# DLRM tower on one core: one-hot steps over 512 columns of four tiles, integer compare of ids, the last chunk in an order of its own

## The chip, the cores and the metric

One core of a Trainium2 chip. The metric is device time in microseconds (us) of one execution. TensorE is called PE (PEld is its weight load), VectorE DVE, ScalarE ACT, GpSimd POOL, SyncE SP. The program runs all engines side by side; they meet at semaphores only.

## The reference

```python
# ids: 2048 samples x 26 tables; 10 of the tables have 1000 rows ("one-hot" here), 16 others
# have 1250 to 125000 rows; every row has 128 float32
e = jnp.stack([tbl_0[ids[:, 0]], ..., tbl_25[ids[:, 25]]], axis=1)   # 2048 x 26 x 128
combined = jnp.concatenate([e, r_dense_x[:, None, :]], axis=1)       # 2048 x 27 x 128
z = jnp.einsum('bfd,bgd->bfg', combined, combined)[:, I, J]          # the 351 pairs f < g
h = jnp.concatenate([z, r_dense_x], axis=1)                          # 2048 x 479
h = jnp.maximum(h @ W_top1 + b_top1, 0.0)                            # 479 x 512
h = jnp.maximum(h @ W_top2 + b_top2, 0.0)                            # 512 x 256
y = h @ W_top3                                                       # 256 x 1
```

## The kernel before

The 2048 samples are 16 tiles of 128, and a chunk is two tiles (256 samples); there are 8 chunks, c = 0 to 7. Tile n is tile t of chunk c with n = 2c + t.

**Gathered tables.** For the 16 large tables POOL issues one indirect DMA per tile and table (`gather`, L242), 256 in all, into one of three row buffers. They are issued in halves of a tile (8 DMAs); from the sixth half on, half b waits until PE has done the half b - 4 of the pair products (`s_gpart`), and the first few halves wait for counts of used one-hot units (`LEAD`). PE turns four tables at a time over the diagonal (`turn`, L521, four transposes: a "turn"), and ACT copies each turn into `xt` (`evac_group`, L360). Turn g = 0 to 3 of a tile needs the landing of the tile's gathers 4g to 4g + 3.

**One-hot tables.** The ten small tables lie in SBUF whole, as a float32r high part (ACT, `high`) and a low part (DVE subtraction, `low`, L304). Their rows are fetched by matmul: partition p holds rows 8p to 8p + 7, ACT turns the chunk's ids (int32, broadcast to 128 partitions by DMA) into `id - 8p` as float (`shift_ids`), DVE compares that with k = 0 to 7, which makes one "unit" each (`make_units`, L279, 128x512 for a pair of tables by 256 samples), and PE multiplies table slices by the units into one of three PSUM banks `ps_lk` (`lookup`, L509: 8 values of k, 2 tables, 2 parts = 32 matmuls of 256 columns for a pair). The first lookup (L489) uses the raw float32 table. Five pairs make a chunk. Eight units are the ring; DVE may overwrite two of them when the matmuls that used them are done (`s_unit_used`). ACT copies each bank to `xt` (`evac_pair`, L350).

**Pair products and the MLP.** `gram` (L536) makes the 27x27 products of a tile in two halves of 64 samples, with 64 short matmuls (128 records) a half; DVE transposes and packs them (`pack`, L287 to L295); PE transposes the pairs (`turn_pairs`, L549), ACT copies them to `zt` (`evac_zt`). `layer1` (L562), `layer2` (L569), `layer3` (L577) follow for the whole chunk, in the next chunk's loop; in the last chunk `last1`, `last2`, `last3` (L590, L597, L605) do it tile by tile.

Every engine's order is written out by hand. In PE's loop for chunk c stand: pair transposes of chunk c-1, turn 3 of tile 2c, layer 3, lookups 3 and 4, layer 1, `gram` of tile 2c, lookup 0 of chunk c+1, the turns of tile 2c+1 between layer 1 parts, lookup 1 of c+1, layer 2, `gram` of tile 2c+1, with turns 0 to 2 of tile 2c+2 and lookup 2 of c+1 among it.

Of the kernel before, what the change touches and what calls it, by code (L numbers as in the profile page):

```python
# [13 lines left out]
P = 128  # L14
# [4 lines left out]
CT = 2  # L19
CHUNKS = TILES // CT  # L20
CS = CT * P
Q = 32
# [11 lines left out]

DENSE = 26
# [6 lines left out]
ROW_BUFS = 3  # L42
# [9 lines left out]
MLP_USES = T1 + T2 + 1  # L52


LP = NO // 2
LB = 3

RING = 8
UNITS = LP * KT
USE = 2  # L60
assert PAIRS == NF * (NF - 1) // 2 and NO % 2 == 0 and RING == KT and KT % USE == 0

CUT = (0, 4, NO)
# [3 lines left out]
LEAD = (0, 2, 8, 14, 20)  # L67

SPLIT = list(range(2, NO)) + [0, 1]
# [4 lines left out]
def build(nc, t_, out):  # L74
    ctx = ExitStack()
    with ctx:
# [11 lines left out]
        xt = sb("xt", [P, CS, NF])  # L88
        dense_x = sb("dense_x", [P, CS])
        ids = [sb(f"ids{h}", [P, CUT[h + 1] - CUT[h], CS], I32) for h in range(2)]  # L90
        ids_from = sb("ids_from", [P, NO, CS])
        onehot = sb("onehot", [P, RING, 2, CS], F32R)
        table = sb("table", [P, NO, 2, KT, D], F32R)
        first_i = sb("first_i", [P, 1], I32)
        first = sb("first", [P, 1])
# [16 lines left out]
        RAWS = len(stage) - 2  # L112
        raw = [stage[j] if j < 2 else stage[2 + (j - 2) % RAWS] for j in range(NO)]

        ps_lk = [pb(f"ps_lk{i}", [P, 2, CS]) for i in range(LB)]
        ps_tr = pb("ps_tr", [P, 512])
# [5 lines left out]
        s_ids = [sem(f"s_ids{h}") for h in range(2)]  # L122
        s_from = sem("s_from")
        s_ids_a = sem("s_ids_a")
        s_from_a = sem("s_from_a")
# [10 lines left out]
        s_first = sem("s_first")  # L136
# [18 lines left out]
        s_carrier = {e: sem(f"s_carrier_{e}") for e in ("dve", "pool", "sp")}  # L155

        def bank(c, i):
            return ps_lk[(c * LP + i) % LB]

        def mlp_bank(n):  # L160
            return (ps_mlp, ps_zt)[n % 2]

        def last1_bank(t, j):
            return ps_lk[j][:, 0, 0:P] if j < LB else (ps_tr, ps_mlp)[t][:, 0:P]

        def last2_bank(t, j):
            return ((ps_tr, ps_zt)[j][:, 0:P], ps_lk[j][:, 0, 0:P])[t]

        def last3_bank():
            return ps_lk[2][:, 0, :]  # L170
# [4 lines left out]
        def _(sp):  # L175
            def load_first_ids():
                sp.dma_start(ids[0][:, 0:2, :].rearrange("p a s -> p (a s)"),
                             t_["ids_onehot"][0:1, 0:2 * CS].to_broadcast([P, 2 * CS])).then_inc(s_ids_a, 16)
# [4 lines left out]
            def load_ids(c, h):  # L183
                if c > 0:
                    sp.wait_ge(s_from, (c - 1) * 2 + h + 1)
                    sp.sem_inc(s_carrier["sp"], 1)
# [537 lines left out]
```

## Time and profile before

| | us |
|---|---|
| median of 3 runs (lowest, highest) | 373.63 (371.1, 375.01) |
| the profiled execution, its own time | 374.13 |
| its span, first to last instruction | 371.9 |
| PE busy | 345.5 (93%) |
| POOL busy | 258.8 (70%) |
| ACT busy | 184.4 (50%) |
| DVE busy | 170.1 (46%) |

The span lies 2.23 us under the time of its own execution. Busy shares are means over the whole span; a gap of an engine counts only where something later waits for it. The page does not count the time in which POOL prepares the next issue as busy.

### The profile page before, as it was taken

Reading aid. Unit: us, or ns where it says so; the run is one execution under the profiler, and the core shown is the slowest. Engines: PE = TensorE matmul, PEld = TensorE weight load, DVE = VectorE, ACT = ScalarE, POOL = GpSimd, SP = SyncE. Lnnn points to the kernel's source line nnn. Section 1 sums busy time; section 2 is a strip of 40 time slices with the busy share of each in tenths; the row PEclk is TensorE's granted clock in tenths of the full one; section 3 lists DMA queues with packets and bytes.
Section 4 is the critical chain, followed back from the end, with each engine's and each line's share of the span. In section 5 each row is a group of like instructions: output and inputs, shape, how many; then the busy total and the mean of one; then the engine's idle time right before and its main releaser. Section 6 shows DMA issues by size and latency. Waiting matters only on the chain.

```text
span 371.9 us, 13580 instructions
## 1 busy us (share of the span) xinstructions
PE 345.5 (93%) x6176; PEld 317.1 (85%) x6176; DVE 170.1 (46%) x380; ACT 184.4 (50%) x235; POOL 258.8 (70%) x265
## 2 busy tenths in 40 slices
PE   1998787989998999999999999999999999999997
PEld 0898776879897889999899998999899998899887
DVE  4589654533533435356245535356244635350220
ACT  3588242764345543473716643473725734376433
POOL 6688877777777777777777777777777777774000
PEclk9999899999998999999999999999999999999999
DMA  7967743211622126221262226321262222221000
GB/s 242 356 183 243 232 149 107 67 51 51 196 70 67 51 58 183 78 65 51 68 198 53 65 54 173 91 67 53 51 206 60 64 53 65 55 56 37 19 4 3
DMA packets 15917, 37.14 MB, mean 100 GB/s; under 512 B 5141, under 2 KB 7829, under 8 KB 15860
## 3 DMA queue, kind: packets, MB, share of 16 engines
q0 software_dynamic: 8192, 16.79, 16.9%
q1 hardware_dynamic: 7668, 19.48, 16.1%
q8 instruction: 49, 0.80, 0.9%
q14 instruction: 8, 0.07, 0.1%
HBM read 36.24 MB, written 0.01 MB: 97 GB/s over the span
## 4 chain that ended last, share of the span: by engine, by line
PE 69%; POOL 20%; issue 7%; DMA 3%; SPq 0%; ACT 0%
PE ps_lk L509 29%; POOL rows L242 20%; PE ps_gram L536 10%; PE ps_tr L521 6%; PE ps_zt L562 6%; PE ps_mlp L562 6%; PE ps_mlp L569 3%; PE ps_zt L569 3%; DMA zt<-in_tbl 2%; PE ps_mlp L577 1%; PE ps_lk L590 1%; PE ps_lk L489 1%; PE ps_zt L549 1%; DMA rows<-in_tbl,gather_ids 1%; PE ps_lk L597 0%
## 5 line engine op out<-in xcount | busy, mean ns | idle before, releaser
L242 POOL DMA_INDIRECT rows<-in_tbl,gather_ids x256 | 257.4, 1006 | 80.4 <-issue 76.2
L279 DVE TENSOR_SCALAR onehot<-ids_from 128x512 fp32r<-128x512 f32 x320 | 126.3, 446 | 94.1 <-PE ps_lk L509 68.7
L509 PE MATMUL ps_lk<-onehot,table 128*128 128x256 f32 x1248 | 163.3, 290 | 2.6 <-DVE onehot L279 2.0
L509 PEld LDWEIGHTS ps_lk<-onehot,table 128*128 128x128 f32 x1248 | 155.9, 196 | 4.3 <-issue 3.1
L360 ACT COPY xt<-ps_tr 128x512 f32<-128x512 f32 x64 | 77.0, 1203 | 93.0 <-PE ps_tr L521 91.2
L536 PEld LDWEIGHTS ps_gram<-xt 128*26 128x26 f32 x4096 | 44.1, 103 | 23.4 <-issue 20.7
L536 PE MATMUL ps_gram<-xt 128*26 128x26 f32 x4096 | 52.7, 192 | 9.8 <-issue 4.8
L350 ACT COPY xt<-ps_lk 128x512 f32<-128x512 f32 x40 | 48.9, 1236 | 14.5 <-PE ps_gram L536 10.5
L287 DVE STREAM_TRANSPOSE zs<-ps_gram 128x832 f32<-128x832 f32 x16 | 16.8, 1050 | 85.9 <-PE ps_gram L536 85.9
L521 PE MATMUL ps_tr<-ident,rows 128*128 128x128 f32 x256 | 39.3, 276 | 3.3 <-ACT xt L360 1.8
L521 PEld LDWEIGHTS ps_tr<-ident,rows 128*128 128x128 f32 x256 | 29.6, 140 | 7.1 <-ACT xt L360 2.4
L562 PE MATMUL ps_zt<-zt,w 128*128 128x256 f32 (+1 forms) x112 | 26.5, 379 | 0.0
L562 PE MATMUL ps_mlp<-zt,w 128*128 128x256 f32 (+1 forms) x112 | 26.5, 379 | 0.0
L562 PEld LDWEIGHTS ps_mlp<-zt,w 128*128 128x128 f32 (+1 forms) x112 | 20.2, 190 | 2.2
L562 PEld LDWEIGHTS ps_zt<-zt,w 128*128 128x128 f32 (+1 forms) x112 | 20.2, 190 | 2.2
L345 ACT ACTIVATE ids_from<-ids,first 128x1536 f32<-128x1536 int32 (+1 forms) x15 | 20.5, 1367 | 1.3 <-DMA ids<-in_ids_onehot 1.3
L377 ACT ACTIVATE h<-ps_mlp,cols 128x256 f32<-128x256 f32 x7 | 3.3, 474 | 27.0 <-PE ps_mlp L569 27.0
L489 PE MATMUL ps_lk<-onehot,h 128*128 128x256 f32 x16 | 6.3, 483 | 8.3 <-DMA h<-in_tbl 8.3
L365 ACT COPY zt<-ps_zt 128x256 f32<-128x256 f32 x16 | 6.5, 407 | 14.6 <-PE ps_zt L549 14.6
L569 PE MATMUL ps_mlp<-h,w 128*128 128x256 f32 x56 | 13.3, 380 | 0.1
L569 PE MATMUL ps_zt<-h,w 128*128 128x256 f32 x56 | 13.3, 381 | 0.0
L304 DVE TENSOR_TENSOR table<-w,table 128x1024 fp32r<-128x1024 f32 x8 | 9.6, 1217 | 4.7 <-ACT table L334 4.7
(57 smaller groups left out, 153.7 us busy)
## 6 DMA issues: line engine op xcount, KB each, us to landing
ids<-in_ids_onehot SPq DMA_DIRECT2D x8, 768.0 KB
w<-in_tbl SPq DMA_DIRECT2D x8, 512.0 KB, 5.0
rows<-in_tbl,gather_ids POOLq DMA_INDIRECT x256
ids<-in_ids_onehot SPq DMA_DIRECT2D x7, 512.0 KB
dense_x<-in_dense SPq DMA_DIRECT2D x8, 128.0 KB
zt<-in_dense SPq DMA_DIRECT2D x8, 128.0 KB
ids<-in_ids_onehot SPq DMA_DIRECT2D x2, 256.0 KB, 4.1
h<-in_tbl SPq DMA_DIRECT2D x1, 512.0 KB, 5.9
```

The lines of the kernel that those rows point to most:

```text
L242: pool.indirect_dma_start(rows[n % ROW_BUFS][:, r, :], None, t_[f"tbl_{GATHERED[r]}"], bass.IndirectOffsetOnAxis(ap=gather_ids[:, n, r:r + ...
L279: nc.vector.tensor_scalar(onehot[:, u % RING, :, :], ids_from[:, 2 * i:2 * i + 2, :], float(k), None, ALU.is_equal).then_inc(s_unit, 1)
L287: nc.vector.transpose(zs[:, :, :], ps_gram[:, :, 0:GS].rearrange("p s g -> p g s")).then_inc(s_zs, 1)
L345: nc.scalar.activation(ids_from[:, CUT[h]:CUT[h + 1], :], ids[h][:, :, :], ACT.Identity, bias=first[:, :]).then_inc(s_from, 1)
L350: nc.scalar.copy(xt[:, :, NG + 1 + 2 * i:NG + 3 + 2 * i].rearrange("p s f -> p f s"), bank(c, i)[:, :, :]).then_inc(s_lk, 1)
L360: nc.scalar.copy(xt[:, t * P:(t + 1) * P, a:a + n].rearrange("p s f -> p f s"), ps_tr[:, 0:n * P].rearrange("p (f s) -> p f s", f=n)).then ...
L489: m = nc.tensor.matmul(bank(0, 0)[:, j, :], raw[j][:, k, :], onehot[:, k, j, :].bitcast(F32), start=(k == 0 and j == 0), stop=(k == KT - 1 ...
L509: m = nc.tensor.matmul(bank(c, i)[:, j, :], table[:, 2 * i + j, part, k, :], onehot[:, u % RING, j, :], start=(k == 0 and j == 0 and part ...
L521: i = nc.tensor.transpose(ps_tr[:, k * P:(k + 1) * P], rows[n % ROW_BUFS][:, r, :], ident[:, :])
L536: i = nc.tensor.matmul(ps_gram[q * Q:q * Q + GS, s, 0:GS], xt[:, x, 0:GS], xt[:, x, 1:NF], start=True, stop=True)
L562: i = nc.tensor.matmul(mlp_bank(j)[:, 0:CS], w1[0:r, k, j * P:(j + 1) * P], zt[0:r, k, :], start=(k == 0), stop=(k == NZ))
L569: i = nc.tensor.matmul(mlp_bank(T1 + j)[:, 0:CS], w2[:, k, j * P:(j + 1) * P], h1[:, k, :], start=(k == 0), stop=(k == T1 - 1))
```

## The change

A step now covers one table for four tiles (512 samples: `XT` = 4 tiles, `N` = 512 columns) instead of two tables for two tiles. Two sets of five tables alternate: chunk 0 makes FIRST for tiles 0 to 3 and, in three narrower steps, SECOND for tiles 0 and 1 (8 steps); chunk 1 makes SECOND for tiles 2 to 5, chunk 2 FIRST for tiles 4 to 7, and so on (5 steps each); chunk 7 has the three narrower SECOND steps alone. That is 41 steps of 8 units against 40. A wide step has 16 matmuls of 512 columns. `xt` holds four tiles, the row buffers are two instead of three. DVE compares the int32 ids with a float32 number per partition, `own[:, k]` = 8p + k, so ACT's shifts and `ids_from` are gone. The ids come in one DMA of 256 KB per step into four buffers; SP waits for the units of step e - 4 before it issues ids e. In the first chunk each step is preceded by the `high` and `low` of the next table or tables only. In chunk 7, layer 2 of chunk 6 and the last chunk's first tile are moved ahead of turn 3 of tile 15.

```diff
+CT = 2
+CS = CT * P
+XT = 2 * CT
+N = XT * P
+FIRST, SECOND = list(range(HALF)), list(range(HALF, NO))
+BY_CHUNK = [tuple(SECOND[i:i + 2]) for i in range(0, HALF, 2)]
+    if c == 0:
+        STEPS += [(c, XT, (i,)) for i in FIRST] + [(c, CT, b) for b in BY_CHUNK]
+    elif c == CHUNKS - 1:
+        STEPS += [(c, CT, b) for b in BY_CHUNK]
+    else:
+        STEPS += [(c, XT, (i,)) for i in (SECOND if c % 2 else FIRST)]
...
-ROW_BUFS = 3
+ROW_BUFS = 2
...
-LEAD = (0, 2, 8, 14, 20)
+LEAD = (0, 2, 6, 12, 20)
...
+            def load_ids(e):
+                if e >= IDS:
+                    sp.wait_ge(s_unit, (e - IDS + 1) * KT)
+                    sp.sem_inc(s_carrier["sp"], 1)
+                sp.dma_start(ids[e % IDS][:, :], t_["ids_onehot"][e:e + 1, :].to_broadcast([P, N])
+                             ).then_inc(s_ids[e % IDS], 16)
...
             sp.dma_start(gather_ids[:, :, :], ...).then_inc(s_gids, 16)
+            load_ids(0)
+            load_raw(0)
+            load_raw(1)
+            load_ids(1)
+            load_raw(2)
+            load_ids(2)
+            load_raw(3)
+            load_ids(3)
+            load_raw(4)
+            for e in range(IDS, IDS + 4):
+                load_ids(e)
+                load_raw(e + 1)
...
-            pool.iota(first_i[:, :], pattern=[[0, 1]], base=0, channel_multiplier=-KT).then_inc(s_const, 1)
+            pool.iota(own_i[:, :], pattern=[[1, KT]], base=0, channel_multiplier=KT).then_inc(s_const, 1)
...
-                    nc.vector.tensor_scalar(onehot[:, u % RING, :, :], ids_from[:, 2 * i:2 * i + 2, :],
-                                            float(k), None, ALU.is_equal).then_inc(s_unit, 1)
+            def make_units(e):
+                dve.wait_ge(s_ids[e % IDS], (e // IDS + 1) * 16)
+                for k in range(KT):
+                    if k % USE == 0 and e > 0:
+                        dve.wait_ge(s_unit_used, ((e - 1) * KT + k) // USE + 1)
+                    w = STEPS[e][1] * P * len(STEPS[e][2])
+                    nc.vector.tensor_scalar(onehot[:, k, 0:w], ids[e % IDS][:, 0:w], own[:, k:k + 1], None, ALU.is_equal
+                                            ).then_inc(s_unit, 1)
...
+            make_units(0)
+            for e in range(1, STEP0[1]):
+                for n in range(len(STEPS[e][2])):
+                    low(STEPS[e][2][n] - 1)
+                make_units(e)
...
+            def evac(e):
+                _, w, tables = STEPS[e]
+                a, f = NG + 1 + tables[0], len(tables)
+                act.wait_ge(s_unit_used, (e + 1) * KT // USE)
+                if w == XT:
+                    nc.scalar.copy(xt[:, :, a], ps_lk[e % LB][:, :]).then_inc(s_lk, 1)
...
+                    for j, i in enumerate(tables):
+                        x = slice(j * w * P, (j + 1) * w * P)
                         for part in range(2):
+                            m = nc.tensor.matmul(ps_lk[e % LB][:, x], table[:, i, part, k, :], onehot[:, k, x],
+                                                 start=(k == 0 and j == 0 and part == 0),
+                                                 stop=(k == KT - 1 and part == 1), skip_group_check=True)
...
+            lookup(5)
+            lookup(6)
+            turn(1, 0)
+            lookup(7)
+            e = STEP0[1]
+            gram(0, 0)
+            lookup(e)
+            turn(1, 1)
+            gram(0, 1)
+            turn(1, 2)
+            turn(1, 3)
+            gram(1, 0)
+            lookup(e + 1)
+            gram(1, 1)
+            lookup(e + 2)
...
...
+            c, a, e = CHUNKS - 1, TILES - 2, STEP0[-2]
+            turn_pairs(a - 2)
+            turn(a, 3)
+            layer3(c - 2)
+            lookup(e + 1)
+            turn_pairs(a - 1)
+            lookup(e + 2)
+            layer1(c - 1, 0)
+            gram(a, 0)
+            turn(a + 1, 0)
+            layer1(c - 1, 1)
+            turn(a + 1, 1)
+            layer1(c - 1, 2)
+            gram(a, 1)
+            layer1(c - 1, 3)
+            turn(a + 1, 2)
+            layer2(c - 1, 0)
+            layer2(c - 1, 1)
+            turn_pairs(a)
             layer3(c - 1)
             last1(0, 0)
             last1(0, 1)
+            turn(a + 1, 3)
+            gram(a + 1, 0)
             last1(0, 2)
+            gram(a + 1, 1)
             last1(0, 3)
+            last2(0, 0)
+            turn_pairs(a + 1)
+            last2(0, 1)
             for j in range(T1):
                 last1(1, j)
+            for j in range(T2):
+                last2(1, j)
             last3()
```

## Rows read from the trace of the kernel before

**Rows 1.** The page: busy tenths of two engines in 40 slices.

```profile
PE   1998787989998999999999999999999999999997
...
POOL 6688877777777777777777777777777777774000
```

**Rows 2.** The page, costliest groups: gathers, one-hot units, lookups, group copies, id shifts.

```profile
L242 POOL DMA_INDIRECT rows<-in_tbl,gather_ids x256 | 257.4, 1006 | 80.4 <-issue 76.2
...
L279 DVE TENSOR_SCALAR onehot<-ids_from 128x512 fp32r<-128x512 f32 x320 | 126.3, 446 | 94.1 <-PE ps_lk L509 68.7
...
L509 PE MATMUL ps_lk<-onehot,table 128*128 128x256 f32 x1248 | 163.3, 290 | 2.6 <-DVE onehot L279 2.0
...
L360 ACT COPY xt<-ps_tr 128x512 f32<-128x512 f32 x64 | 77.0, 1203 | 93.0 <-PE ps_tr L521 91.2
...
L345 ACT ACTIVATE ids_from<-ids,first 128x1536 f32<-128x1536 int32 (+1 forms) x15 | 20.5, 1367 | 1.3 <-DMA ids<-in_ids_onehot 1.3
```

**Rows 3.** The timeline of POOL: gathers 8, 9, 240 and 256 of 256.

```profile
12.40 0.95 POOL L242 DMA_INDIRECT rows<-in_tbl,gather_ids  x1 [0.30 <-issue]
...
15.19 0.94 POOL L242 DMA_INDIRECT rows<-in_tbl,gather_ids  x1 [1.85 <-PE ps_lk L489]
...
318.47 0.94 POOL L242 DMA_INDIRECT rows<-in_tbl,gather_ids  x1 [0.30 <-issue]
...
338.95 0.94 POOL L242 DMA_INDIRECT rows<-in_tbl,gather_ids  x1 [0.30 <-issue]
```

**Rows 4.** The chain in order of time (start, us, what): a landing, a lookup, layer 2.

```profile
111.75 2.93 DMA rows<-in_tbl,gather_ids
...
142.34 3.83 PE ps_lk L509 x32
...
315.63 1.73 PE ps_mlp L569 x8
```

**Rows 5.** The timeline of PE: fourth transposes of tiles 4, 14 and 15.

```profile
114.81 0.63 PE L521 MATMUL ps_tr<-ident,rows 128*128 128x128 f32 x4 [1.53 <-DMA rows<-in_tbl,gather_ids]
...
328.24 0.60 PE L521 MATMUL ps_tr<-ident,rows 128*128 128x128 f32 x4
...
348.54 0.60 PE L521 MATMUL ps_tr<-ident,rows 128*128 128x128 f32 x4
```

**Rows 6.** The timeline of the start: units, first lookup, subtractions, a gather, a slow lookup.

```profile
6.15 2.97 DVE L279 TENSOR_SCALAR onehot<-ids_from 128x512 fp32r<-128x512 f32 x8 [4.08 <-ACT ids_from L338]
...
8.26 1.19 PE L489 MATMUL ps_lk<-onehot,h 128*128 128x256 f32 x2 [8.26 <-DMA h<-in_tbl]
...
25.52 2.35 DVE L304 TENSOR_TENSOR table<-w,table 128x1024 fp32r<-128x1024 f32 x2
...
26.73 1.97 POOL L242 DMA_INDIRECT rows<-in_tbl,gather_ids  x1 [0.30 <-PE ps_lk L509]
...
41.45 5.38 PE L509 MATMUL ps_lk<-onehot,table 128*128 128x256 f32 x32 [0.71 <-DVE onehot L279]
...
46.76 1.69 PE L536 MATMUL ps_gram<-xt 128*26 128x26 f32 x128
```

**Rows 7.** Busy time by stretch: stretch, length, PE busy, granted clock, DMA share, GB/s.

```profile
42.00:44.00 2.00, 2.00 (x12) 0.50 0.91 276
```

**Rows 8.** The timeline of the last 24 us, PE, ACT and DVE.

```profile
349.27 1.99 PE L569 MATMUL ps_mlp<-h,w 128*128 128x256 f32 x8
...
351.19 1.27 PE L536 MATMUL ps_gram<-xt 128*26 128x26 f32 x128
...
356.65 1.05 DVE L287 STREAM_TRANSPOSE zs<-ps_gram 128x832 f32<-128x832 f32 x1 [7.93 <-PE ps_gram L536]
...
358.40 0.40 DVE L295 COPY_PREDICATED packed<-lower,zs 128x169 f32<-128x169 int32 x1
...
361.53 2.84 PE L590 MATMUL ps_lk<-zt,w 128*128 128x128 f32 x24
...
368.67 1.23 PE L605 MATMUL ps_lk<-cols,h 128*128 128x1 f32 x8
```

More of the change, by code:

```diff
@@ L52 @@
 MLP_USES = T1 + T2 + 1
[L55 removed]
+assert PAIRS == NF * (NF - 1) // 2 and NO % 2 == 0
+RING = KT
+USE = 2
 LB = 3
[L58 to L63, printed above, removed]
+IDS = 4
 PARTS = 2
[L67 to L69 removed]
+LEAD = (0, 2, 6, 12, 20)
+SPLIT = list(range(1, NO)) + [0]
 LAST = (CHUNKS - 1) * MLP_USES
@@ L121, in build @@
         s_gids = sem("s_gids")
[L122 to L125, printed above, removed]
+        s_ids = [sem(f"s_ids{b}") for b in range(IDS)]
         s_densex = sem("s_densex")
@@ L329, in _ @@
+            make_units(STEP0[-2] + 2)
+            pack(TILES - 2)
+            pack(TILES - 1)
         @block.scalar
@@ L389, in last_relu2 @@
             def last_relu2(t, j):
-                act.wait_ge(s_mlp, LAST + CT * T1 + t * T2 + j + 1)
+                act.wait_ge(s_mlp, last(t) + T1 + j + 1)
                 nc.scalar.activation(h2[:, j, t * P:(t + 1) * P], last2_bank(t, j), ACT.Relu,
                                      bias=cols[:, T1 + j:T1 + j + 1]).then_inc(s_act, 1)
-            act.wait_ge(s_first, 1)
-            nc.scalar.activation(warm[:, :], first[:, :], ACT.Identity)
-            shift_first(0, 2, s_ids_a, s_from_a)
@@ L413, in _ @@
-            shift_ids(1, 0)
-            evac_group(0, 1, 0)
-            evac_group(0, 1, 1)
-            shift_ids(1, 1)
-            evac_group(0, 1, 2)
-            evac_group(0, 1, 3)
+            act.wait_ge(s_own, 1)
+            nc.scalar.activation(warm[:, :], own[:, 0:1], ACT.Identity)
+            high(0)
+            high(1)
+            evac(0)
+            evac_group(0, 0)
+            high(2)
+            evac(1)
+            high(3)
+            evac(2)
+            evac_group(0, 1)
@@ L482, in lookup_first @@
             def lookup_first():
+                pe.wait_ge(s_raw[0], 16)
                 for k in range(KT):
                     pe.wait_ge(s_unit, k + 1)
-                    for j in range(2):
-                        if k == 0:
-                            pe.wait_ge(s_raw[j], 16)
-                        m = nc.tensor.matmul(bank(0, 0)[:, j, :], raw[j][:, k, :], onehot[:, k, j, :].bitcast(F32),
-                                             start=(k == 0 and j == 0), stop=(k == KT - 1), skip_group_check=True)
+                    m = nc.tensor.matmul(ps_lk[0][:, :], raw[0][:, k, :], onehot[:, k, :].bitcast(F32),
+                                         start=(k == 0), stop=(k == KT - 1))
@@ L677, in _ @@
             last1(0, 1)
-            turn_pairs(c, 1)
+            turn(a + 1, 3)
+            gram(a + 1, 0)
             last1(0, 2)
+            gram(a + 1, 1)
             last1(0, 3)
+            last2(0, 0)
+            turn_pairs(a + 1)
+            last2(0, 1)
             for j in range(T1):
                 last1(1, j)
-            for t in range(CT):
-                for j in range(T2):
-                    last2(t, j)
+            for j in range(T2):
+                last2(1, j)
             last3()
```

475 lines of the change are left out of this document (226 added, 249 removed).

## The prediction

> **What bounds the kernel now.** I read the page first: PE is at nine tenths or more nearly throughout, POOL at seven to eight tenths until it stops at some 340 us [rows 1]. The grouped rows [rows 2] correct the second: POOL's 256 gathers are 257.4 us busy and have 80.4 us of idle time before them, 76.2 of it under "issue", which is no wait for anybody. So POOL works for 257.4 + 76.2 = 333.6 us, as much as PE's 345.5. Its timeline says the same: apart from 1.85 us ahead of the ninth gather it never stands, and the last one starts at 338.95 [rows 3]. From gather 80 at 111.75 [rows 4] to gather 240 at 318.47 [rows 3] lie 160 gathers in 206.7 us, 1.292 us each, 41.3 us for a chunk of 32.
>
> How far is PE behind? A gather's rows land 2.93 us after its start [rows 4]. Turn 3 of tile 4 waits 1.53 us for them at 114.81. Turn 3 of tile 14 comes at 328.24 [rows 5], its rows are there at 318.47 + 2.93 = 321.4; turn 3 of tile 15 comes at 348.54, its rows at 341.9. PE needs (328.24 - 114.81) / 5 = 42.7 us a chunk against POOL's 41.3, and by the end it is 6.8 us behind. So at most about 7 us can be had from PE's lookups before POOL takes over, and what follows the last rows has to be counted by itself.
>
> **The change part by part.**
>
> *Wider lookups.* 32 lookup matmuls of 256 columns take 3.83 us [rows 4], 119.7 ns each; 256 columns at 2.4 GHz are 106.7, so 13 are on top. If the 13 belong to the instruction, 512 columns take 226 ns; if they go with the columns, 239; if the weight load hides wholly, 213. A step of 16 then takes 3.62 us (3.41 to 3.83), and a chunk of five saves 1.0 us (0 to 2.1). I take the middle. The Trainium skill ("TensorE: Matmul & The Clock Gate", Back-to-back issue gap) gives a warm gap of N/2.4 + 2.5 ns, 216 ns for 512 columns, which would save 1.9 us a chunk; the 119.7 measured here for 256 columns is 10 over that rule, so I don't lean on it. It doesn't matter much, as the sum shows.
>
> *Moved lookups.* Chunk 7's first five tables come with chunk 6's four-tile steps. PE's loop 6 loses two lookups (7.7 us), loop 7 half a lookup (1.9 us), and chunk 0 gains two and a half. There PE waits anyway: 1.53 us at tile 4 in the end, and for DVE and ACT before.
>
> *Start.* One 256 KB id load fewer lies ahead of the first raw table, so the first matmul starts some 0.7 us before the 8.26 of now [rows 6], and DVE doesn't wait for ACT's shift. The ninth gather waits for half of the first lookup; now that costs 1.85 - 0.3 = 1.5 us [rows 3], and the new first lookup needs one table instead of two (now it stops a second time for the other). I put POOL 1.3 us earlier. Then the steps: a DVE set of eight units is 2.97 us, two subtractions 2.35 [rows 6]. Steps 1 to 4 cost DVE 4.2 us each, 5 and 6 some 5.4, 7 about 3.5, against 3.6, 3.8 and 1.9 on PE; from 17.6 us PE gets through lookup 7 at about 44.6, the first `gram` from 46 to 48, one lookup, and the second half ends near 54 (now 48.4 [rows 6]). POOL's sixth half, near 60, waits for it: 6 us of room. Entering loop 1 PE is 1 us later than now and at tile 4's turn 3 still ahead of its rows, having 1.5 us to spare now plus a loop of saving. Cost: nothing; with that cover gone, each us late is a us on POOL.
>
> *POOL.* Its instructions are the same; the third row buffer was not used as such, since half b waits for half b - 4 before and after. Subtractions lengthen gathers (1.97 us where two of them run [rows 6], 0.94 otherwise); their number stays, and 328 unit operations instead of 320, more of them early, may add 0.5 us.
>
> *DVE's compare.* int32 input and a per-partition number in place of float and an immediate. A unit of 512 elements is 2.97 / 8 = 371 ns [rows 6], while a subtraction takes 1175 ns for 1024 elements, so the compare goes at a faster rate than one element in the subtraction's time; no row shows this operation with an int32 input. Lower bound 371 (it reads as many bytes), upper the subtraction's rate, half of 1175 ns and up to 90 ns of fixed cost that doesn't halve, 590 to 680 for 512 (an estimate). I take 371: the nearest row is the same instruction on words of the same size. "VectorE: DVE Perf Modes" (What auto-detection actually checks) in the Trainium skill names source count, place and outer size for the two-port mode, not the type, and so sides with 371; no row here shows it.
>
> *ACT* loses its id shifts (20.5 us and two small ones [rows 2]); it stands 91 us waiting for PE's turns, so that is worth nothing to the end. SP's id loads wait for units four steps back; the raw tables 6 to 9 are queued behind them, but are issued when their buffers come free anyway, some 5 us before they are used.
>
> *Loop 7 and the end.* Turn 3 of tile 14 waits for rows: 321.4 - 1.3 + 0.5 + 0.1 = 320.7. In every case of the lookup price PE is there first: it needs five chunks of 42.7 from 114.8, less 7.7 and 5 savings of 0 to 2.1 (two steps fewer in the last), at 312 to 320.6. From there to the end of turn 2 of tile 15 the work is that of now less half a lookup: 20.3 - 1.9 = 18.4 us. New ahead of turn 3 of tile 15: 0.23 until layer 1's last activation is done, layer 2 twice 1.75 [rows 4], 0.75 for its activation (now hidden behind `gram`), pair transposes and layer 3 1.2, two parts of `last1` 1.8: 7.5. That gives 25.9. PE idles some 5 to 8 us of the 12 before. In the trace of now the first `gram`, whose PE had waited just before, is followed by a stretch at clock 0.50 [rows 7], that is 1.2 GHz, in which a lookup takes 5.38 us [rows 6], some 1.3 more than undisturbed; after a longer idle time I add 1.5.
>
> After turn 3 of tile 15: transposes and the ACT copy until `gram` 2.0; `gram`, `last1` part, `gram` 1.2 + 0.9 + 1.2 [rows 8]; DVE's pack from its transpose at 356.65 to the last copy's end at 358.8 [rows 8], 2.15, and 0.25 to notice the `gram`; pair transposes and ACT copies 1.5 with their hand-overs; `last1` for tile 15 four times 0.9; activation 0.75; `last2` 1.8 [rows 8]; from there to the end as now, 371.9 - 368.67 = 3.2 [rows 8]. Sum 18.6, plus 0.8 for a clock drop that may follow the idle 1.5 us.
>
> Total: 320.7 + 25.9 + 1.5 + 18.6 + 0.8 = 367.5, against a span of 371.9: -4.4. The profiled execution took 374.13, so 369.7; its time lies 0.5 above the median of 373.63, which gives **369.2**.
>
> **The rivals.** *POOL has less to fight* (0.15): fewer gathers meet DVE's early subtractions (spread singly now), no clock drop in loop 7 or the tail. Each of the two is worth 2 to 3 us: 364 to 367. For it speaks that 1.292 a gather stands over the 0.94 + 0.30 = 1.24 of an undisturbed one [rows 3]; against it, that DVE's operations are as many as before.
>
> *The compare runs at one element per cycle* (0.10), the slower side. Units take 650 ns, eight of them 5.2 us. DVE then sets chunk 0: step 7's units end near 57, the next set near 63, the second half of the first `gram` near 65, 5 us after POOL wants it, and PE reaches tile 4 some 13 us later than now. Later loops hold 26 us of units in 41 and lose about 1 us each, so tile 14 comes at 327 instead of 320.7, and the time is 369.2 + 6.5 = 376, to 380 if POOL's delay adds. It decides from a unit of about 500 ns, where chunk 0's slack is used. The "GPSIMD Engine Reference" of the Trainium skill says that VectorE's two-port operations contend with GpSimd; by that, POOL would run faster at the same time, which only softens this case.
>
> *The last order costs more than it hides* (0.25): PE runs the 7.5 us of layer 2 and `last1` ahead of turn 3 while its rows, landed at 341, wait until 346.6. If the clock stays down longer, or the hand-overs of the tail (each 0.2 to 0.75, six of them) are dearer, 2 to 4 us go: 371 to 373, no change. *It doesn't matter where the lookups are* because PE is late at tile 4: would need 5 us more in chunk 0 than I count; it is within the case before.
>
> **How the numbers follow.** Main case 0.50, 367 to 371 with 369.2 the likeliest. 0.15 lies at 364 to 367, 0.25 at 371 to 373, 0.10 at 376 to 380. The range of 8 in 10 goes from 365 to 375. One per cent is about what a measurement of this kernel tells from no change: under 369.9 fall most of the better half of the main case and the first rival, 0.15 + 0.37 = 0.52; within one per cent 0.40; over 377.4 0.08.
>
> **What would show it.** Unit near 371 ns; a 512-column matmul 213 to 239 ns apart; gathers still 1.29 us apart, the last one near 338; PE's waits for rows at turns 1 to 3 of tile 14, some 8 us together or less; turn 3 of tile 15 near 348, 5 us after its rows; 19 us from there to the end. I am wrong if POOL waits for `gram` in the first 70 us, if units take over 500 ns, or if POOL's spacing moves by 2%.

## The result and the profile after

| | before | after |
|---|---|---|
| median of 4 runs (lowest to highest), us | 374.32 (371.1 to 645.01) | 385.86 (385.28 to 388.19) |
| span of the profiled execution, us | 371.9 | 383.5 |
| turn 3 of tile 14 / of tile 15, start | 328.24 / 348.54 | 330.65 / 357.88 |
| last gather, start | 338.95 | 347.76 |

One of the four runs before took 645.01 us, far off the others (371.1 to 375.01), and the ratio leaves it out. The ratio is 1.0335, 95% interval 1.0294 to 1.0376: slower by 3.3%, where 369.2 us was forecast, and outside the range of 365 to 375. The page of the kernel after, its parts 2 (40 slices), 4 (the chain that ended last) and 5 (groups: instructions and busy time, mean ns, idle time before them and its releaser), beside [rows 1] and [rows 2]:

```profile
POOL 6788877777777777777777777777777777772000
PEclk9999995999998799999999999999999998999959
...
POOL 60%; issue 19%; PE 17%; DMA 2%; ACT 1%; DVE 0%; SPq 0%
...
L262 POOL DMA_INDIRECT rows<-in_tbl,gather_ids x256 | 267.8, 1046 | 78.9 <-issue 77.1
L297 DVE TENSOR_SCALAR onehot<-ids,own 128x512 fp32r<-128x512 int32 (+1 forms) x328 | 141.8, 490 | 80.5 <-PE ps_lk L547 72.2
...
L558 PE MATMUL ps_tr<-ident,rows 128*128 128x128 f32 x256 | 41.2, 285 | 10.9 <-DMA rows<-in_tbl,gather_ids 9.5
```

POOL is the bound: the chain runs along its gathers for 79% of the span (60 + 19 "issue"). They are the same 256 as before, but the mean is 1046 ns instead of 1006 [rows 2]. The last starts 8.8 us later. Of that 6.2 us are lost early: the first 32 take 53.9 us from the first one's start to the 33rd's, against 47.7. The other 2.6 us come in the 223 gathers after that, 1.303 us apart against 1.292, where DVE makes units and no subtractions any more. At the end of its gathers the chain passes from POOL to PE here (its pieces: start, us, what), and PE's timeline says the same: at turn 3 of tile 14 it had waited 1.54 us for rows.

```profile
327.67 2.84 DMA rows<-in_tbl,gather_ids
330.51 0.14 issue
330.65 0.63 PE ps_tr L558 x4
```

The early loss has a place. POOL's timeline of the kernel after, 28 to 40 us (start, us, instruction, idle before it):

```profile
28.95 1.28 POOL L262 DMA_INDIRECT rows<-in_tbl,gather_ids  x1 [0.30 <-PE ps_lk L547]
30.53 3.55 POOL L262 DMA_INDIRECT rows<-in_tbl,gather_ids  x1 [0.30 <-issue]
34.39 1.28 POOL L262 DMA_INDIRECT rows<-in_tbl,gather_ids  x1 [0.30 <-issue]
35.98 3.55 POOL L262 DMA_INDIRECT rows<-in_tbl,gather_ids  x1 [0.30 <-issue]
```

and DVE's over the same time:

```profile
27.65 3.25 DVE L297 TENSOR_SCALAR onehot<-ids,own 128x512 fp32r<-128x512 int32 x8
30.82 1.21 DVE L303 TENSOR_TENSOR table<-zt,table 128x1024 fp32r<-128x1024 f32 x1
31.96 1.22 DVE L303 TENSOR_TENSOR table<-w,table 128x1024 fp32r<-128x1024 f32 x1
33.09 3.25 DVE L297 TENSOR_SCALAR onehot<-ids,own 128x512 fp32r<-128x512 int32 x8
36.26 2.35 DVE L303 TENSOR_TENSOR table<-w,table 128x1024 fp32r<-128x1024 f32 x2
```

Eight units take 3.25 us, 406 ns each, against 371 [rows 6]. A gather that begins 0.29 us before two subtractions takes 3.55 us. In the kernel before, the gather that begins 0.19 us before two of them (at 25.33; its line stands under "Open" below) takes 1.09, and only the next, which begins within the second, takes 1.97 [rows 6]. The long one ends at 30.53 + 3.55 = 34.08, and the subtractions end at 31.96 + 1.22 = 33.18: 0.90 us later, as long as an undisturbed gather lasts (0.94). From one set of units to the next DVE takes 33.09 - 27.65 = 5.44 us, and POOL the same from one long gather to the next (35.98 - 30.53 = 5.45). In that time it gets two gathers out, where undisturbed, at 0.94 + 0.30 us each, it would get four.

The wide lookups do what they were to do, at the dear end. PE's timeline in the middle of the run (x16 are the 16 matmuls of a step):

```profile
212.92 3.92 PE L547 MATMUL ps_lk<-onehot,table 128*128 128x512 f32 x16
216.67 1.90 PE L600 MATMUL ps_mlp<-zt,w 128*128 128x256 f32 x8
```

A step is 216.67 - 212.92 = 3.75 us, 234 ns a matmul, against 3.83 for 32 narrow ones [rows 4].

The end of the program, PE's timeline from turn 3 of tile 15 (the last number is the idle time before the group and its releaser):

```profile
357.88 0.60 PE L558 MATMUL ps_tr<-ident,rows 128*128 128x128 f32 x4
359.78 1.21 PE L573 MATMUL ps_gram<-xt 128*26 128x26 f32 x123 [1.30 <-issue]
363.09 0.24 PE L573 MATMUL ps_gram<-xt 128*26 128x26 f32 x5 [2.10 <-issue]
363.26 1.18 PE L628 MATMUL ps_lk<-zt,w 128*128 128x128 f32 x8
364.38 1.59 PE L573 MATMUL ps_gram<-xt 128*26 128x26 f32 x115
366.82 0.39 PE L573 MATMUL ps_gram<-xt 128*26 128x26 f32 x13 [0.85 <-issue]
367.14 2.08 PE L628 MATMUL ps_mlp<-zt,w 128*128 128x128 f32 x8
```

Within each half of the pair products PE stands and waits for no semaphore that the trace shows ("issue"), 2.10 and 0.85 us. And the clock falls after the first of these pauses; windows of the same stretch (length, busy of PE, PEld, DVE, ACT, POOL, then the granted clock as a share of 2.4 GHz, DMA share, GB/s):

```profile
360.00:363.00 3.00, 0.99 (x120) 0.88 (x104) 0.00 (x0) 0.00 (x0) 0.00 (x0) 1.00 0.02 5
363.00:366.00 3.00, 2.88 (x128) 2.57 (x128) 0.00 (x0) 0.37 (x1) 0.00 (x0) 0.71 0.03 5
366.00:369.00 3.00, 2.18 (x21) 2.05 (x21) 1.57 (x2) 0.00 (x0) 0.00 (x0) 0.50 0.00 0
```

Eight matmuls of `last1` take 1.18 us at 363.26 and 2.08 at 367.14. From turn 3 of tile 15 to the end are 25.6 us; the forecast had 18.6 + 0.8, the kernel before takes 23.4.

### The profile page after: what moved, and what is told of

It reads as the page before. It is cut to its first block, busy times and chain, and to the rows that moved or that the text cites. A ratio compares the mean times of both kernels' runs of the same rounds, so it can differ in the third digit from the quotient of the medians.

```text
span 383.5 us, 12513 instructions
## 1 busy us (share of the span) xinstructions
PE 349.1 (91%) x5616; PEld 289.8 (76%) x5616; DVE 184.9 (48%) x388; ACT 166.6 (43%) x219; POOL 269.1 (70%) x265
## 4 chain that ended last, share of the span: by engine, by line
POOL 60%; issue 19%; PE 17%; DMA 2%; ACT 1%; DVE 0%; SPq 0%
POOL rows L262 60%; PE ps_lk L547 4%; PE ps_lk L523 3%; PE ps_gram L573 2%; PE ps_lk L628 2%; DMA ids<-in_ids_onehot 1%; PE ps_zt L600 1%; PE ps_mlp L600 1%; PE ps_tr L558 1%; DMA rows<-in_tbl,gather_ids 1%; PE ps_tr L636 1%; PE ps_lk L636 1%; PE ps_mlp L628 1%; PE ps_mlp L607 1%; PE ps_zt L607 0%
## 5 line engine op out<-in xcount | busy, mean ns | idle before, releaser
L262 POOL DMA_INDIRECT rows<-in_tbl,gather_ids x256 | 267.8, 1046 | 78.9 <-issue 77.1
L297 DVE TENSOR_SCALAR onehot<-ids,own 128x512 fp32r<-128x512 int32 (+1 forms) x328 | 141.8, 490 | 80.5 <-PE ps_lk L547 72.2
L547 PE MATMUL ps_lk<-onehot,table 128*128 128x512 f32 (+1 forms) x704 | 157.2, 377 | 1.6 <-DVE onehot L297 1.6
L547 PEld LDWEIGHTS ps_lk<-onehot,table 128*128 128x128 f32 x704 | 121.8, 192 | 23.3 <-ACT xt L369 1.6
L573 PEld LDWEIGHTS ps_gram<-xt 128*26 128x26 f32 x4096 | 44.9, 105 | 24.8 <-issue 21.5
L366 ACT COPY xt<-ps_lk 128x512 f32<-128x512 f32 x35 | 42.1, 1240 | 27.3 <-PE ps_gram L573 13.8
L558 PE MATMUL ps_tr<-ident,rows 128*128 128x128 f32 x256 | 41.2, 285 | 10.9 <-DMA rows<-in_tbl,gather_ids 9.5
L558 PEld LDWEIGHTS ps_tr<-ident,rows 128*128 128x128 f32 x256 | 31.0, 144 | 18.5 <-issue 9.8
L523 PE MATMUL ps_lk<-onehot,h 128*128 128x512 f32 x16 | 9.8, 782 | 7.3 <-DVE onehot L297 7.3
L523 PEld LDWEIGHTS ps_lk<-onehot,h 128*128 128x128 f32 x16 | 4.0, 257 | 12.2 <-issue 11.0
L607 PEld LDWEIGHTS ps_mlp<-h,w 128*128 128x128 f32 x56 | 10.5, 189 | 2.3 <-ACT h L392 0.7
```

What stands on the lines that cost most here:

```text
L262: pool.indirect_dma_start(rows[n % ROW_BUFS][:, r, :], None, t_[f"tbl_{GATHERED[r]}"], bass.IndirectOffsetOnAxis(ap=gather_ids[:, n, r:r + ...
L297: nc.vector.tensor_scalar(onehot[:, k, 0:w], ids[e % IDS][:, 0:w], own[:, k:k + 1], None, ALU.is_equal).then_inc(s_unit, 1)
L366: nc.scalar.copy(xt[:, :, a], ps_lk[e % LB][:, :]).then_inc(s_lk, 1)
L523: m = nc.tensor.matmul(ps_lk[0][:, :], raw[0][:, k, :], onehot[:, k, :].bitcast(F32), start=(k == 0), stop=(k == KT - 1))
L547: m = nc.tensor.matmul(ps_lk[e % LB][:, x], table[:, i, part, k, :], onehot[:, k, x], start=(k == 0 and j == 0 and part == 0), stop=(k == ...
L558: i = nc.tensor.transpose(ps_tr[:, k * P:(k + 1) * P], rows[n % ROW_BUFS][:, r, :], ident[:, :])
```

## The experiments

Four edits, alone and together: the compare's per-partition number, the input's type, the subtractions, and the last order. The first nine runs fell on chips where the kernel before takes 482 to 507 us. PE stands within the pair products there without a semaphore to wait for, 76.3 us in all in e1 against 4.8 in the kernel before on the first chip; that it lacks instructions is the reading that e10 to e13 below support. Durations of single DVE and POOL instructions can be read from these runs, and their ratios hold for such a chip. The last eight are on a chip where it takes 373.8 to 373.9. Ratios are to the kernel before as measured beside each run, with 95% intervals. "Starved" marks the first kind of chip below.

**The per-partition number, put into the kernel before** (e1, e5, e14):

```diff
+            pool.iota(kk_i[:, :], pattern=[[1, KT]], base=0, channel_multiplier=0)
+            nc.vector.tensor_copy(kk[:, :], kk_i[:, :])
...
-                                            float(k), None, ALU.is_equal)
+                                            kk[:, k:k + 1], None, ALU.is_equal)
```

> The kernel before with one difference: the compare takes k from a per-partition float32 number instead of an immediate; ids stay float32. Theory A (the pointer costs the 35 ns by which a unit is longer after the change, 406 against 371, and with it the longer gathers): units 406 ns, undisturbed-loop gathers 1.00 to 1.03 us on average instead of 0.985, gathers beside a pair of subtractions over 3 us instead of 1.97, time 374 to 380. Theory B (the int32 input costs it): units 371 ns, gathers and time as before, 373 to 375.

> The same kernel as the first experiment (the kernel before, k from a per-partition number), on a chip on which PE's pair products don't wait for their instructions. Theory A, whose unit time of 406 us/1000 is shown already: POOL's gathers are longer, the last one starts 5 to 9 us later than 339, time 376 to 381. Rival: POOL's delay is caught before it reaches the end, since PE is 7 us behind the rows there: time 373 to 375.

> The kernel before with k taken from a per-partition number, once more, now on a chip where the kernel before takes 374 us. The pointer took 12.9 us of the changed kernel in the form with few instructions. If it acts through POOL's gathers alone: the start loses 4 to 6 us, the rest 1 to 2 us, and PE's 7 us of lateness hide part: 376 to 380. If the time stays within 2 us of 374, the pointer only costs where DVE has the moved lookups too.

Starved: 1.0246 [1.0083, 1.0409] and 1.0137 [0.9973, 1.0301]. On the other chip 1.0171 [1.0112, 1.023], span 376.4. This one edit reproduces the pattern of the kernel after. The timelines of e14, DVE's:

```profile
28.40 3.25 DVE L283 TENSOR_SCALAR onehot<-ids_from,kk 128x512 fp32r<-128x512 f32 x8
31.57 2.35 DVE L312 TENSOR_TENSOR table<-w,table 128x1024 fp32r<-128x1024 f32 x2
```

and POOL's:

```profile
29.69 1.28 POOL L245 DMA_INDIRECT rows<-in_tbl,gather_ids  x1 [0.30 <-issue]
31.28 3.55 POOL L245 DMA_INDIRECT rows<-in_tbl,gather_ids  x1 [0.30 <-issue]
```

The first 32 gathers take 53.7 us (6.0 more than before), those after them stand 1.310 us apart against 1.292, the mean of all is 1048 ns, and the last starts at 349.10, 10.2 us later than before. The span grows by 4.5 only: PE was 6.8 us behind its rows there, which hides the rest.

**The type alone** (e2): in the kernel before, `ids_from` becomes int32, k stays an immediate.

```diff
-        ids_from = sb("ids_from", [P, NO, CS])
+        ids_from = sb("ids_from", [P, NO, CS], I32)
```

> The kernel before with one difference: ACT writes the shifted ids as int32 and the compare reads int32 with the immediate k. Theory A (the pointer is the cost): units 371 ns, time as before. Theory B (the int32 input is the cost): units 406 ns and gathers lengthened, time 374 to 380.

1.003 [0.995, 1.0111]; the first 32 gathers take 48.5 us. Its DVE timeline:

```profile
35.23 2.87 DVE L279 TENSOR_SCALAR onehot<-ids_from 128x512 fp32r<-128x512 int32 x8
```

2.87 / 8 = 359 ns a unit, and the kernel before has the same 2.87 in that stretch: int32 costs nothing.

**The subtractions** (e3): in the kernel after, the low part of each table is filled with zeros in place of the difference; the tables lose their low part, the transfers stay.

```diff
-                nc.vector.tensor_tensor(table[:, j, 1, :, :], raw[j][:, :, :],
-                                        table[:, j, 0, :, :].bitcast(F32), ALU.subtract)
+                nc.vector.memset(table[:, j, 1, :, :].bitcast(F32), 0.0)
```

> The changed kernel with the subtraction that makes the low table parts replaced by a memset to zero on the same engine: the low parts are left out, the instruction count and order stay, and a memset of 1024 elements takes about as long (1.1 us against 1.2) but reads nothing. Theory C (gathers are lengthened by DVE's reads while it runs without a pause from 18 to 46 us, above all by the subtractions): no gather over 2 us, gather 33 starts near 50 instead of 57, and the time falls by 4 to 8 us, since POOL sets it. Rival D (the gathers are slowed by the DMA traffic of tables and ids at the start): gathers as in the changed kernel, gather 33 at 57, time within 1 us.

Starved, 0.979 [0.957, 1.0006]; the kernel after itself has 0.9807 on such a chip (e9, below), so the time says nothing. No gather from 14 to 48 us is over 1.16 us, and the 33rd starts at 52.3. It looks as if the long gathers needed the subtractions, but DVE's stream is another one here. Windows of the kernel after, of e3 and of the kernel before (length, busy of PE, PEld, DVE, ACT, POOL, granted clock, DMA share, GB/s):

```profile
18.00:48.00 30.00, 27.55 (x269) 23.89 (x268) 30.00 (x61) 21.18 (x22) 25.43 (x16) 1.00 0.56 161
...
18.00:48.00 30.00, 16.47 (x61) 10.84 (x60) 12.33 (x25) 8.80 (x9) 21.21 (x21) 0.82 0.46 131
...
18.00:48.00 30.00, 26.42 (x405) 24.95 (x405) 24.82 (x50) 18.21 (x18) 24.21 (x20) 0.94 0.74 228
```

In e3 DVE is busy 12.33 us of the 30, as a memset takes 0.91 us (1.1 was expected) and, above all, PE frees the units late; in the kernel after it never stops. Only from 52 us on does DVE of e3 run its units nearly without a pause, and there gathers are long with no subtraction anywhere (DVE's timeline, then POOL's):

```profile
56.58 0.91 DVE L303 MEMSET table<- 128x1024 f32 x1 [0.16 <-issue]
57.42 3.13 DVE L297 TENSOR_SCALAR onehot<-ids,own 128x512 fp32r<-128x512 int32 x8
...
56.62 2.06 POOL L262 DMA_INDIRECT rows<-in_tbl,gather_ids  x1 [0.30 <-issue]
64.13 2.07 POOL L262 DMA_INDIRECT rows<-in_tbl,gather_ids  x1 [0.30 <-issue]
```

So a gather can take 2.07 us beside pointer units and memsets alone, and whether 3.55 needs the subtractions this run doesn't show. The rival "transfers at the start slow the gathers" falls by the kernel before: it moves more in the same stretch (share 0.74 against 0.56) and has no gather over 1.97 us.

**The old last order** in the kernel after (e4, e6, e16): in chunk 7 layer 2 of chunk 6 and the four `last1` parts of tile 14 go back behind turn 3 of tile 15.

```diff
+            turn(a + 1, 3)
+            gram(a + 1, 0)
+            gram(a + 1, 1)
+            for j in range(T1):
+                last1(0, j)
+            last2(0, 0)
...
-            last1(0, 0)
-            last1(0, 1)
-            turn(a + 1, 3)
-            gram(a + 1, 0)
-            last1(0, 2)
-            gram(a + 1, 1)
-            last1(0, 3)
-            last2(0, 0)
```

> The changed kernel with the last chunk's order of before: turn 3 of tile 15 right after layer 1, its pair products between the two parts of layer 2, no last-layer work ahead of them. Theory E (the new last order holds turn 3 back 7 us behind its rows, and its close-set pair products run into issue gaps and the half clock): turn 3 of tile 15 at 351, right behind its rows, 23 to 24 us from there to the end, time about 377. Rival F (the tail's issue gaps and clock drop come with the changed program whatever the order): 25 to 27 us from turn 3 to the end, time 379 to 381. Rival G (the old order only gives back what the new one hides): 385.

> The same kernel as the fourth experiment (the changed kernel with the last chunk's order of before). Theory E: turn 3 of tile 15 at 351, right behind its rows, 23 to 24 us from there to the end, time 376 to 378. Rival F (issue gaps and clock drop come whatever the order): 379 to 381. Rival G (the order only moves the time): 385.

> The changed kernel with the last chunk's order of before, all products computed. In the form with few instructions this gave 1.6 us. If issue gaps and half clock at the end come from the new order: 376 to 379, 24 us or less from turn 3 of tile 15 to the end. If they come anyway: 383 to 385.

Starved: 0.9761 [0.9587, 0.9936] and 0.9756 [0.9608, 0.9904]. On the other chip 1.0115 [1.006, 1.0169], 2.2 points under the kernel after (the two were not measured side by side). Turn 3 of tile 14 comes as there (330.90), turn 3 of tile 15 20.9 us later, then 24.1 to the end: 45.0 us from the one to the end against 52.8. PE's timeline of e16 at the end, without a gap inside the halves; over the 24.1 us the granted clock is 1.00, against 0.80 in the kernel after:

```profile
354.45 1.27 PE L571 MATMUL ps_gram<-xt 128*26 128x26 f32 x128
355.64 1.99 PE L605 MATMUL ps_zt<-h,w 128*128 128x256 f32 x8
357.57 1.45 PE L571 MATMUL ps_gram<-xt 128*26 128x26 f32 x128
```

**An immediate in the kernel after** (e7, e15; with the old last order as well: e8, e17). ACT subtracts 8p from the ids in place, in int32, as the kernel before did into a float copy:

```diff
+            def shift(e):
+                act.wait_ge(s_ids[e % IDS], (e // IDS + 1) * 16)
+                nc.scalar.activation(ids[e % IDS][:, :], ids[e % IDS][:, :], ACT.Identity, bias=first[:, :])
...
-                    nc.vector.tensor_scalar(..., ids[e % IDS][:, 0:w], own[:, k:k + 1], None, ALU.is_equal)
+                    nc.vector.tensor_scalar(..., ids[e % IDS][:, 0:w], float(k), None, ALU.is_equal)
```

> The changed kernel, but ACT makes id - 8p in place (int32) and the compare has its immediate k again; steps, orders and tiles stay those of the change. If the pointer is what slows POOL: units 360 ns, no gather over 2.2 us, the last gather starts at 339 to 341 instead of 348; the end follows it by 5 to 8 us: time 378 to 381. If the moved lookups alone crowd DVE at the start, gathers of 3 us stay and the time is 383 to 386.

> Both of the last two edits together, so what is left of the change is the steps of 512 columns, the moved lookups and the id loads. If the two costs are separate they add: the last gather starts at 340, turn 3 of tile 15 comes at 344 to 347, the time is 369 to 372, under the kernel before. If the wide steps or the moved lookups have a cost of their own: 374 or more.

> The changed kernel with ACT making id - 8p in place and the immediate compare, all products computed. If the 12.9 us of the reduced form carry over: 372 to 375, the last gather at 338 to 341. If 378 to 381: part of the gain of the reduced form lay in the pair products.

> Both edits, all products computed: wide steps, moved lookups and id loads are what is left of the change. Additive: 366 to 370, below the kernel before. If the last order of before gives nothing once the rows come early: 372 to 375.

Starved: e7 0.9879 [0.9809, 0.9949], e8 0.9696 [0.9553, 0.9839]; against the 0.9807 of e9 neither tells an effect of the operand. On the other chip e15 0.9963 [0.9921, 1.0005] and e17 0.981 [0.9757, 0.9863], median 366.78. So e17, with both parts undone, is faster than both kernels. Its grouped rows:

```profile
L263 POOL DMA_INDIRECT rows<-in_tbl,gather_ids x256 | 257.5, 1006 | 78.8 <-issue 77.7 <-DMA gather_ids<-in_ids_gather 1.1
L298 DVE TENSOR_SCALAR onehot<-ids 128x512 fp32r<-128x512 int32 (+1 forms) x328 | 126.4, 440 | 103.6 <-ACT ids L364 49.8 <-PE ps_lk L564 46.4 <-PE ps_lk L540 2.8
```

and its POOL timeline around a gather that meets two subtractions:

```profile
33.48 1.09 POOL L263 DMA_INDIRECT rows<-in_tbl,gather_ids  x1 [0.30 <-issue]
34.88 1.89 POOL L263 DMA_INDIRECT rows<-in_tbl,gather_ids  x1 [0.31 <-issue]
37.07 1.16 POOL L263 DMA_INDIRECT rows<-in_tbl,gather_ids  x1 [0.30 <-issue]
```

The gather's mean is 1006 ns again, as before, the first 32 take 46.1 us, none over 1.89 from 18 to 48 us, though DVE has the same instructions in the same order and hardly a pause either (busy 28.67 us of the 30 from 18 to 48). DVE's period is 5.06 us (26.89 to 31.95 and 31.95 to 37.00 in its timeline), and POOL gets three gathers out in it instead of two. What tells it from the kernel after in this stretch is the operand (and ACT's shift); e15, with the last order of the kernel after, shows the same (47.0 us, none over 1.97).

**The kernel after, unedited, on a starved chip** (e9):

> The changed kernel itself, unedited, so that the edits made to it have a run of it beside them on the same chip. If this chip is like that of the first comparison (before near 374): 386, a ratio of 1.03. If it is like that of the experiments so far (before near 490, PE waiting some 140 us for the instructions of the pair products): the ratio is under 1, since the change takes 1067 instructions away, 480 to 486 against 490.

0.9807 [0.9744, 0.9871]: there the same change is faster by 1.3 to 2.6%. Waits of e9 (engine, what it waited for, us in total, times, longest):

```profile
POOL rows L262 <- PE ps_gram L573: 91.4, 27, 9.2
...
PE ps_gram L573 <- issue: 70.6, 98, 2.5
```

POOL waits 91 us for the pair products, so dearer gathers can hide there. That the kernel gains because it has a thousand instructions fewer (12513 against 13580) fits, but no run shows it.

**Few instructions in the pair products** (e10 to e13). Each half is two matmuls of 338 columns (four records) in place of 64 short ones; most products are left out, the time that PE is busy with a half stays 1.3 us:

```diff
-                for s in range(part * (Q // PARTS), (part + 1) * (Q // PARTS)):
-                    for q in range(QUADS):
-                        i = nc.tensor.matmul(ps_gram[q * Q:q * Q + GS, s, 0:GS], xt[:, x, 0:GS],
-                                             xt[:, x, 1:NF], start=True, stop=True)
+                s = part * (Q // PARTS)
+                for q in range(2):
+                    i = nc.tensor.matmul(ps_gram[0:GS, s:s + 13, 0:GS], xt[:, x, 0:GS],
+                                         xt[:, x:x + 13, 1:NF], start=True, stop=True)
```

> On this chip PE waits some 70 us for the instructions of the pair products, which hides POOL's limit. So each half of a tile's pair products (64 matmuls of 26 columns) is replaced by 2 matmuls of 338 columns that take the same 1.15 us; most of the products are left out, all else stays. Kernel before in this form: PE is no longer starved, POOL runs without stopping at 1.29 us a gather, time 368 to 378 as on the first chip. If it stays above 420, PE is starved elsewhere too.

> The changed kernel with the same replacement of pair products (most of them left out). If the loss is in POOL's gathers and the order at the end, it comes back: last gather at 346 to 349, 5 to 9 us later than in the kernel before in this form, and the time 5 to 9 us above that kernel. If the 12 us of the first chip came from issue gaps of the pair products at the end, the difference shrinks to 3 us or less.

> The same as the last, with the immediate compare (ACT makes id - 8p in place). If the pointer is what slows POOL: last gather 6 to 9 us earlier than in the changed kernel of this form, time 5 to 9 us less. If the moved lookups slow it: no more than 2 us less.

> The changed kernel in this form with the last chunk's order of before (pointer compare kept). If holding turn 3 of tile 15 back by 7 us is a cost of its own: 3 to 5 us less than the changed kernel of this form. If the new order pays as I predicted and only the issue gaps and the clock spoiled it: 0 to 2 us more.

| with few instructions | ratio [95%] | last gather | turn 3 of 14, of 15 | from there to the end |
|---|---|---|---|---|
| e10, before | 0.976 [0.9725, 0.9796] | 340.25 | 322.61, 342.98 | 22.7 |
| e11, after | 1.0209 [1.0158, 1.026] | 351.96 | 334.53, 360.73 | 18.7 |
| e12, immediate | 0.9877 [0.9827, 0.9926] | 336.46 | 318.88, 348.08 | 18.6 |
| e13, old last order | 1.0152 [1.0081, 1.0223] | 350.96 | 333.55, 353.55 | 23.8 |

In this form the old last order gives 0.6 of a point (e13 against e11, 1.6 us), and the intervals overlap. From turn 3 of tile 14 to the end are 43.8 us in e13 and 44.9 in e11. The end of e12 on PE:

```profile
349.97 1.30 PE L592 MATMUL ps_gram<-xt 128*26 128x338 f32 x4 [1.30 <-issue]
...
352.29 1.32 PE L592 MATMUL ps_gram<-xt 128*26 128x338 f32 x4
353.54 1.16 PE L647 MATMUL ps_mlp<-zt,w 128*128 128x128 f32 x8
```

The gaps of 2.10 and 0.85 are gone, `last1` keeps 1.16, and the end takes the 18.6 us that the forecast summed. The operand's price doesn't hang on the short matmuls: 1.0209 - 0.9877 = 3.3 points here, and 3.0 between e16 and e17 (1.0115 - 0.981), each pair measured side by side.

## Why the prediction was wrong, point by point

**The failed step is "DVE's compare".** It asked what the int32 input does, and there it was right (359 ns in e2, with an immediate). The rule of the Trainium skill that it cited there ("VectorE: DVE Perf Modes", What auto-detection actually checks) agrees with that. It took the per-partition number as free, "the nearest row is the same instruction on words of the same size". That operand costs 35 to 47 ns a unit (406 against 371 or 359). The large part is elsewhere: on POOL, whose gathers get longer beside such units. 6.2 us are lost in the first chunk, where units and subtractions alternate, and 2.6 us later beside units alone (those gathers take 998 ns on average against 987). The step *POOL* allowed "0.5 us" for all of it; the last gather starts 8.8 us later, and turn 3 of tile 14 came 9.9 us later than its 320.7. Taking the number away again (e15) brings the turn to 321.21, half a us from the forecast, and the ratio from 1.0335 to 0.9963, 3.7 points or 13.9 us, of which the profiled spans show 10.9 (383.5 against 372.6). The two ratios weren't measured side by side; the pairs that were, e11 and e12, e16 and e17, give 3.3 and 3.0 points.

The gather that lasts until 0.90 us after the subtractions beside it looks like one that couldn't begin before they had ended. "SBUF — State Buffer" (Who interferes with whom) in the Trainium skill says that VectorE and GpSimd share a pair of ports under an exclusive lock, and that a VectorE instruction in a two-port mode keeps the pair for its whole length; a VectorE instruction with two SBUF inputs, as the subtraction is, contends by it only with GpSimd instructions that read SBUF. The traces agree in so far as no gather of the first chunk that begins within a subtraction (0.05 us or more after its start) ends less than 0.8 us after it, with either operand. The rule doesn't say why the operand matters, and not every gather waits: in the kernel before, the gather at 25.33 begins 0.19 us ahead of a subtraction and is through before that one ends. The prediction had cited a sentence of that kind ("GPSIMD Engine Reference"), but only to soften a rival and not to price the change itself.

**The second is a term of the sum: the end.** Counted 18.6 + 0.8, measured 25.6. Some 3 us are the two gaps in the pair products (2.95), the other 4 come with the low clock after them: 18.6 in e12 and 18.7 in e11, where neither occurs, and 22.7 in e15, which has the gaps (2.13 and 0.70) at a mean clock of 0.92 in place of 0.80. So the work was counted rightly, and the gaps left out. The kernel before has one such gap at its end, 0.69 us, and its clock there is 1.00.

**The last order itself** stood in the sum as a net loss (7.5 us ahead of turn 3, against a shorter end, 18.6 for 23.4), and nothing asked what the version without it would give. In the kernel after, the rows of tile 15 are there at 347.76 + 2.84 = 350.6 and their turn comes at 357.88, 7.3 us later (the forecast's own numbers give 7 from 341 to 348, though it wrote 5); in e16 it comes at 351.80, their rows being there at some 351.2. The rival "the last order costs more than it hides" had the mechanism and was priced 2 to 4 us; undoing it gives 2.2 points (8.2 us, not measured side by side) with the pointer, and 1.5 points (5.7 us, e15 and e17, side by side) without. With few instructions, where the gaps are gone, it gives 1.6 us, which are not clear of noise (e11 and e13). So holding turn 3 back costs little by itself, and most of what the new order costs comes with the gaps and the low clock.

**Refuted:** "POOL has less to fight" (its spacing in the first chunk grew), and "the compare runs at one element per cycle" (406 ns, below the 500 from which it decides; yet its direction, slower, came true by another way). Also "PE idles some 5 to 8 us of the 12": it waited 1.96 us for rows at turn 1 of tile 14 and 1.54 at turn 3, 3.5 together. It had no lead to lose, as the late gathers held it at tile 4 already, whose turn 3 came at 121.83 instead of 114.81.

**Right:** that the ninth gather's wait goes (none is left, but it starts at 14.58 instead of 15.19, 0.6 us earlier and not 1.3), that the second half of the first `gram` ends near 54 (54.4) and POOL doesn't wait for it, the price of the wide lookups (234 ns, within 213 to 239, near the end at which it goes with the columns; the 216 by the rule of the Trainium skill in "TensorE: Matmul & The Clock Gate", Back-to-back issue gap, would have been 18 too low), and that POOL becomes the bound. The 27.2 us from turn 3 of tile 14 to that of tile 15 (forecast 25.9 + 1.5) are luck: the 1.5 stood for a low clock, and the granted clock over this stretch is 1.00; 1.3 us more work than was counted took its place. In e15, where the clock does fall there (0.94), it takes 28.7. The prediction's own sign of error, POOL's spacing moving by 2%, is met over all 256 gathers (1.317 to 1.351 us, 2.6%); between gathers 80 and 240, where the prediction had taken its 1.29, it moved by 0.8% only (1.303).

What the rest of the change is worth can be read from e17: 1.9% (1.4 to 2.4), 7 us, with the wide steps, the moved lookups and the earlier start, which reach turn 3 of tile 14 at 319.80 instead of 328.24. The two undone parts cost it 5.2 points (1.0335 - 0.981, not measured side by side).

**Open:** by what way pointer units lengthen a gather. DVE's period differs with the operand (5.06 or 5.44 us), and with the period the moment at which a gather meets a subtraction; slower units with an immediate weren't tried. But the traces show that the moment alone isn't the cause. In the kernel before and the runs with an immediate all 46 gathers of the first chunk that begin within a subtraction end 0.8 to 1.15 us after it. With pointer units 50 do so, and they end 0.8 to 4.4 us after it. Two that begin 0.51 and 0.52 us into one, in e17 (immediate) and in e9 (pointer), each with the subtraction that it meets; the fifth line is the gather of the kernel before at 25.33:

```profile
17.72 1.22 DVE L304 TENSOR_TENSOR table<-w,table 128x1024 fp32r<-128x1024 f32 x1
18.23 1.53 POOL L263 DMA_INDIRECT rows<-in_tbl,gather_ids  x1 [0.31 <-issue]
...
44.94 1.23 DVE L303 TENSOR_TENSOR table<-h,table 128x1024 fp32r<-128x1024 f32 x1
45.46 4.00 POOL L262 DMA_INDIRECT rows<-in_tbl,gather_ids  x1 [0.30 <-issue]
...
25.33 1.09 POOL L242 DMA_INDIRECT rows<-in_tbl,gather_ids  x1 [0.30 <-issue]
```

With pointer units the same moment gives short gathers too: in the kernel after, one that begins 0.51 us into a subtraction, at 22.72, takes 1.62. What decides between the two isn't known. Nor is it shown why PE's instructions come late on some chips far more than on others, and in the new last order, but not in the old one.

## What to carry to other kernels

Before an operand is changed on one engine, ask what the engine next to it is doing at that time and whether that one is the bound: here an operand that made DVE's instruction 35 ns longer, on an engine with half its time free, came with 9 us on POOL, which had none. Where one engine's stream is the bound, read the mean of its instruction, and the long ones one by one, before adding work beside it. And work that is moved ahead of a late arrival is only free until the arrival; compare the order that waits for it with the order that doesn't, as the same sum gives both. Where an edit is to take one thing away from a busy engine, look first whether the engine is still as busy without it: in e3 DVE was busy 12.3 us of a stretch in which it had been busy for 30.

## What the runs showed of the hardware that was not expected

- An is_equal of 512 elements per partition with a per-partition float number takes 406 ns, with an immediate 359 to 371, int32 or float input alike.
- An indirect DMA's issue on POOL takes 0.94 us undisturbed; after the first chunk up to 1.22 beside immediate units and 1.28 beside pointer units; 1.89 to 1.97 when it begins within a subtraction among immediate units; up to 3.55 in the kernel after (5.93 in e1 and e9) among pointer units and subtractions that follow each other without a pause, and up to 2.07 with memsets in place of the subtractions (e3).
- PE can stand within runs of short matmuls with no semaphore to wait for: 2.1 us inside one half of the pair products at the end of the kernel after, 71 us in all in e9 and 76 in e1, on chips where the kernel before takes 30% longer. With two matmuls of 338 columns in place of the 64 the gaps inside the halves at the end are gone (e11 to e13), so its supply of instructions is the likely bound; the trace doesn't show the supply itself.
